# A four-layer graph network on one Trainium2 core: product banks in turn over the graphs' borders, a second buffer for the turned means, mask stores four graphs ahead

## What is computed

```python
adjT = jnp.transpose(adj.astype(jnp.float32), (0, 2, 1))
w = _masked_row_softmax(adjT)              # 1/degree on the edges, 0 elsewhere
region = jnp.matmul(w, features)           # features = h; mean of h over the edges
region = jnp.matmul(region, kernel_1) + bias_1
region = _batch_norm(region, gamma_1, beta_1)
people = jnp.matmul(jnp.transpose(w, (0, 2, 1)), region)
people = jnp.matmul(people, kernel_2) + bias_2
people = _batch_norm(people, gamma_2, beta_2)
x = x + people
```

## Time and profile before

| what | value |
|---|---|
| median of 3 runs | 1524.31 us (1522.05 to 1525.0) |
| profiled execution, its own time | 1522.59 us |
| its span, first to last instruction | 1520.8 us |
| TensorE matmuls busy | 1394.4 us (92%) |
| VectorE busy | 1148.9 us (76%) |
| ScalarE busy | 815.6 us (54%) |
| GpSimd busy | 383.4 us (25%) |
| granted TensorE clock, tenths, 40 slices of 38 us | `9999999799968989999999999999999999999998` |

### The profile page before, as it was taken

One profiled execution on the slowest core, in us unless ns is written; L12 is line 12 of the kernel. 1 busy time (PEld: TensorE's weight loads), 2 busy tenths in 40 slices (PEclk: granted clock), 3 DMA queues, 4 the chain that ended last, 5 costly groups with the idle time before them and its releaser, 6 DMA issues.

```text
span 1520.8 us, 32886 instructions
## 1 busy us (share of the span) xinstructions
PE 1394.4 (92%) x12642; PEld 1258.7 (83%) x12642; DVE 1148.9 (76%) x3270; ACT 815.6 (54%) x1811; POOL 383.4 (25%) x337
## 2 busy tenths in 40 slices
PE   5899999799945888999999999999999999999886
PEld 5899999555535777999999998999999999999785
DVE  4566664687835767888898888888888888887565
ACT  4677777022233454745656556556574565654621
POOL 6334340000010304133132331331313313223120
PEclk9999999799968989999999999999999999999998
DMA  9999992376742122231432323413323143131111
GB/s 206 227 207 213 206 220 64 102 251 234 246 157 56 48 79 84 71 91 52 109 105 64 98 60 99 114 50 105 91 84 92 51 110 105 50 84 46 39 42 43
DMA packets 111839, 169.35 MB, mean 111 GB/s; under 512 B 9808, under 2 KB 61760, under 8 KB 109632
## 3 DMA queue, kind: packets, MB, share of 16 engines
q1 hardware_dynamic: 87264, 125.20, 28.3%
q0 software_dynamic: 19584, 33.56, 12.0%
q10 hardware_dynamic: 4832, 8.45, 1.6%
HBM read 158.74 MB, written 42.00 MB: 132 GB/s over the span
## 4 chain that ended last, share of the span: by engine, by line
PE 46%; DVE 12%; DVEq 4%; ACT 3%; POOL 3%; issue 2%; DMA 0%; ACTq 0%
PE ps L1666 31%; PE ps L1625 3%; PE ps L1648 2%; DVE wts_C L973 2%; PE ps L1593 2%; PE ps L1637 2%; PE ps L1639 2%; PE ps L1638 2%; POOL wts_B L886 1%; DVEq L996 1%; PE ps L1679 1%; DVE xC L1050 1%; DVE wts_A L973 1%; DVEq L1006 1%; DVE st_B L908 1%
## 5 line engine op out<-in xcount | busy, mean ns | idle before, releaser
L1666 PE MATMUL ps<-hV,wts_B 128*128 128x129 f32 x2048 | 252.9, 279 | 13.2 <-POOL wts_B L886 5.4
L886 POOL TENSOR_TENSOR wts_B<-wts_B,off 128x1024 f32<-128x1024 f32 (+7 forms) x128 | 177.9, 1414 | 322.8 <-PE ps L1648 322.8
L1666 PEld LDWEIGHTS ps<-hV,wts_B 128*128 128x128 f32 x2048 | 241.6, 194 | 17.6 <-POOL wts_B L886 7.4
L1666 PE MATMUL ps<-hP_A,wts_A 128*128 128x129 f32 x1920 | 230.9, 275 | 1.2 <-ACT xB L1392 0.7
L1666 PEld LDWEIGHTS ps<-hP_A,wts_A 128*128 128x128 f32 x1920 | 221.5, 191 | 3.8 <-DVE hP_C L957 2.9
L1666 PE MATMUL ps<-hP_C,wts_C 128*128 128x129 f32 x1920 | 220.1, 274 | 0.0
L1666 PEld LDWEIGHTS ps<-hP_C,wts_C 128*128 128x128 f32 x1920 | 217.4, 191 | 0.5
L973 DVE SCALAR_TENSOR_TENSOR wts_A<-row_A,least_A,ring_A 128x1024 f32<-128x1024 f32 x128 | 161.0, 1275 | 11.3 <-ACT row_A L1347 7.7
L973 DVE SCALAR_TENSOR_TENSOR wts_C<-row_C,least_C,ring_C 128x1024 f32<-128x1024 f32 x120 | 167.0, 1404 | 0.0
L295 ACT ACTIVATE maskT<-ps 128x1024 fp8e4<-128x1024 bf16 x128 | 131.2, 1025 | 56.4 <-PE ps L337 45.2
L349 PE MATMUL ps<-x,adj_b 128*128 128x129 f16 x896 | 121.3, 223 | 15.8 <-ACT whn L278 13.3
(11 more groups left out here) (237 smaller groups left out, 2707.1 us busy)
## 6 DMA issues: line engine op xcount, KB each, us to landing
adj_b<-in_adj POOLq DMA_DIRECT2D x120, 256.0 KB, 10.0
maskT_scratch<-maskT SPq DMA_DIRECT2D x16, 1024.0 KB, 6.9
ring_A<-maskT_scratch SPq DMA_DIRECT2D x64, 256.0 KB, 3.1
off<-maskT_scratch SPq DMA_DIRECT2D x32, 512.0 KB, 6.6
ring_C<-maskT_scratch SPq DMA_DIRECT2D x64, 256.0 KB, 3.3
xa<-in_x SPq DMA_DIRECT2D x16, 512.0 KB, 4.5
whT_scratch<-whT_s ACTq DMA_DIRECT2D x32, 256.0 KB, 6.4
whT_b<-whT_scratch SPq DMA_DIRECT2D x16, 512.0 KB, 4.8
```

Source lines behind the costliest of these rows:

```text
L886: pool.tensor_tensor(w, w, off_fp8[:, k, k * P:N], ALU.mult).then_inc(S["B", "up"], 1)
L1666: last = nc.tensor.matmul(Q_SLOTS[c // 2 % 2][:, c % 2, 0:PW], wts[y][:, j, c * P:c * P + P], src[:, j, :], start=(j == 0), stop=(j == T - 1))
```

## The change

1. The bank of a product is (b * T + c) % 3, in turn over the graphs' borders, and line 343 asks for the division three tiles back everywhere.
2. The halves of the turned means go in turn into `whT_s` and into a second buffer, which is the part of `maskT` for the last two tiles of the last graph. Odd halves of the first 14 graphs use the second one; the last four halves all use `whT_s`. Each buffer has its own semaphore, and ScalarE waits for the last store from the second buffer before it writes the last graph's mask there.
3. SP issues the mask stores of graphs 0 to 3 at the start of the second stage, and then in `save(b)` that of graph b + 4. All on one semaphore, but for graph 0, which has its own.

```diff
-            BANK = [c % 3 for c in range(T)]
             LAG, HT = 3, T // 2
-            psW = [ps[:, 2 + BANK[c], :] for c in range(T)]
+
+            def psW(b, c):
+                return ps[:, 2 + (b * T + c) % 3, :]
...
+            SPARE = 2 * (B - 2)
+            by_spare = [n for n in range(SPARE) if n % 2 == 1]
+            by_own = [n for n in range(2 * B) if n not in by_spare]
+            whT_spare = maskT[:, B - 1, T - 2:T, :].rearrange("p t n -> p (t n)").bitcast(fp32)
...
                         act.wait_ge(a_sums_made, n + 1)
-                        if n > 0:
-                            act.wait_ge(a_whT_out, n * 16)
-                        nc.scalar.copy(whT_s[:, :], psWT[:, h * HALF:(h + 1) * HALF]).then_inc(a_whT_kept, 1)
+                        k, mine, kept = (1, by_spare, whT_spare) if n in by_spare else (0, by_own, whT_s[:, :])
+                        if mine.index(n) > 0:
+                            act.wait_ge(a_whT_out[k], mine.index(n) * 16)
+                        nc.scalar.copy(kept, psWT[:, h * HALF:(h + 1) * HALF]).then_inc(a_whT_kept, 1)
                         act.wait_ge(a_whT_kept, n + 1)
-                        act.dma_start(whT_dram[b, :, h * HALF:(h + 1) * HALF], whT_s[:, :]).then_inc(a_whT_out, 16)
+                        act.dma_start(whT_dram[b, :, h * HALF:(h + 1) * HALF], kept).then_inc(a_whT_out[k], 16)
...
                             act.wait_ge(a_turned, n + 1)
-
+                            if b == B - 1 and c == T - 2:
+                                act.wait_ge(a_whT_out[1], len(by_spare) * 16)
...
-                            if not (first and c < 3):
-                                pe.wait_ge(a_wh, n + 1 - (3 if c >= 3 else 2))
-                            q = psW[c]
+                            if n >= 3:
+                                pe.wait_ge(a_wh, n - 2)
+                            q = psW(b, c)
...
+            b_mask_first, b_mask_out = stage_sem("b_mask_first"), stage_sem("b_mask_out")
+            AHEAD = 4
...
                         if b == B - 1:
-                            sp.wait_ge(a_whT_out, 2 * B * 16)
+                            sp.wait_ge(a_whT_out[0], len(by_own) * 16)
...
+                    def save_mask(b):
+                        sp.dma_start(maskT_dram[b], maskT[:, b, :, :]).then_inc(b_mask_out if b > 0 else b_mask_first, 16)
+
+                    for b in range(AHEAD):
+                        save_mask(b)
+
                     def save(b, par):
-                        sp.dma_start(maskT_dram[b], maskT[:, b, :, :]).then_inc(b_mask_out[par], 16)
+                        if b + AHEAD < B:
+                            save_mask(b + AHEAD)
                         sp.wait_ge(b_pT, b + 1)
...
+                    sp.wait_ge(b_mask_out, (B - 1) * 16)
                     for par in range(2):
-                        sp.wait_ge(b_mask_out[par], B // 2 * 16)
                         sp.wait_ge(b_pT_out[par], B // 2 * 16)
```

More of the change, by code:

```diff
@@ L139, in gnn_stack_kernel @@
             (a_var, a_rstd, a_h, a_turned, a_kept, a_wh_made, a_deg,
-             a_wh, a_sums_made, a_whT_kept, a_whT_out) = (stage_sem(n) for n in (
+             a_wh, a_sums_made, a_whT_kept) = (stage_sem(n) for n in (
                 "a_var", "a_rstd", "a_h", "a_turned", "a_kept", "a_wh_made", "a_deg",
-                "a_wh", "a_sums_made", "a_whT_kept", "a_whT_out"))
+                "a_wh", "a_sums_made", "a_whT_kept"))
+            a_whT_out = [stage_sem(f"a_whT_out{k}") for k in range(2)]
+            SPARE = 2 * (B - 2)
+            by_spare = [n for n in range(SPARE) if n % 2 == 1]
+            by_own = [n for n in range(2 * B) if n not in by_spare]
+            whT_spare = maskT[:, B - 1, T - 2:T, :].rearrange("p t n -> p (t n)").bitcast(fp32)
             psT = [ps[:, k, :].bitcast(bf16) for k in range(2)]
-            BANK = [c % 3 for c in range(T)]
             LAG, HT = 3, T // 2
-            psW = [ps[:, 2 + BANK[c], :] for c in range(T)]
+            def psW(b, c):
+                return ps[:, 2 + (b * T + c) % 3, :]
             psG = ps[:, 5, 0:GW]
@@ L277, in divide @@
                         act.wait_ge(a_deg, b * T + c + 1)
-                        nc.scalar.mul(whn[:, c, 0:P], psW[c][:, 0:P], rdg[:, c:c + 1]).then_inc(a_wh, 1)
+                        nc.scalar.mul(whn[:, c, 0:P], psW(b, c)[:, 0:P], rdg[:, c:c + 1]).then_inc(a_wh, 1)
                     def keep_whT(b, h):
@@ L534, in gnn_stack_kernel @@
             pT_b = sbb("pT_b", [P, 2, N])
-            b_mask_out = [stage_sem(f"b_mask_out{k}") for k in range(2)]
+            b_mask_first, b_mask_out = stage_sem("b_mask_first"), stage_sem("b_mask_out")
+            AHEAD = 4
             b_pT_out = [stage_sem(f"b_pT_out{k}") for k in range(2)]
@@ L563, in _ @@
                             save(k * 2 + par, par)
-                    sp.wait_ge(b_mask_out[0], 16)
+                    sp.wait_ge(b_mask_first, 16)
                     sp.wait_ge(b_pT_out[0], 16)
```

## The result

The changed kernel takes **1506.88 us** (median of 4 runs, 1504.79 to 1508.29), the kernel before 1523.85 us on the same chip (median of 4 runs). The ratio is 0.9892, with a 95% interval of 0.9877 to 0.9906. Forecast were 1507.5 us, 1502 to 1514, and faster with a chance of 0.95: all three hold. The profiled execution took 1508.29 us (span 1506.5), 14.3 us less than that of before.

A forecast was written before the change was run, and what follows sets the result against it. TensorE was taken as the bound in both stages, leaving only its idle time and the stages' ends to win: 1522.59 - 13.3 - 2.5 = 1506.8, or 1508.5 by the median; forecast 1507.5 us, range 1502 to 1514.

The forecast's parts named there:

- First stage: TensorE's waits for ScalarE's division, mostly at graph borders, shrink: 16.1 - 2.8 - 0.4 + 0.4 = 13.3 us gained.
- TensorE only arrives earlier and waits longer: Second graph's 2.77 us wait at 42.86, where VectorE waits for x, stays; the 0.4 us border before it is lost.
- Part 1: Banks over the border: small gaps of 0.35 us go to zero; large ones, up to 2.30 us, keep 0.5 us.
- its mask copies have two banks of room: First stage: ScalarE, busy 125.57 of 160 us, was listed among checks of what is late next.
- Part 2: Second whT buffer: ScalarE's 11.5 us of store waits go, except the last, about 1.4 us, with what the banks leave.
- Start of the second stage: Graph 2's whT load, queued behind four mask stores (10 to 27.6 us), costs 0, with 2 us in the range.
- End of the second stage: Mask stores ahead free the last pTf store; VectorE is last and the next stage starts 2.5 us earlier.
- The transfers set the first stage's pace: Rival, chance 0.12: late x delays h and TensorE waits; 4.9 us of the gain lost, time 1512.4.
- The end is no shorter: Rival, chance 0.08: other transfers keep the queue full at the second stage's end, pTf lands unchanged; time 1510.0.
- The store queue slows the second stage: Rival, chance 0.02: each graph's transfers go one after another, 6.0 us a graph, 78 us over 13 graphs; 1585 in all.
- It does not do what it says: Rival, chance 0.03: first-stage border waits stay because a release other than the division ends them; time 1520 to 1523.
- which comes when it comes: Second graph's x transfer, for which VectorE sat 7.0 us; its landing was taken as given.

The follow-up runs named there:

- e2_buffer: Only the second buffer of the turned means, on the kernel before: 1512.37 us against 1523.12, ratio 0.9927.
- e3_masks: Only the mask stores issued four graphs ahead, on the kernel before: 1520.0 us against 1523.12, ratio 0.9982.
- w_late: Changed kernel with the weights' small loads moved behind the x load of graph 12, two x buffers: 1504.45 us against 1522.7, ratio 0.9874.
- w_last: Changed kernel with the weights' small loads moved behind the last x load of all, two x buffers: 1500.17 us against 1522.51, ratio 0.9848.
- e1_banks: Only the product banks in turn over the borders and the relaxed line 343, on the kernel before: 1518.27 us against 1523.12, ratio 0.997.
- ahead1: Changed kernel with mask stores issued one graph ahead instead of four: 1504.77 us, ratio 0.9889 to the kernel before.
- again: Second profiled execution of the changed kernel, nothing altered: 1502.97 us.
- ahead16: Changed kernel with all sixteen mask stores issued at the start of the second stage: 1524.42 us against 1522.42 for the kernel before, ratio 1.0013.

## Why the prediction was right, and where not

- **The sum** was -13.3 for the first stage, 0 for the second's start and -2.5 for its end, together -15.8; the profiled execution gave -12.1, +0.5 and -2.7, together -14.3. The forecast of 1507.5 against a median of 1506.88 is closer than its terms were, and in part luck: the four executions lie between 1504.79 and 1508.29, and the second profiled execution of the same kernel gives -13.9, -1.8 and -2.7.
- **First stage.** All of the gaps behind the stall went: 16.1 - 2.8 + 0.4 - 0.4 = 13.3 us, as worked out. "TensorE only arrives earlier and waits longer" was right. In this trace the wait ended 0.36 us later and the two tiles behind it took 5.41 us instead of 4.57, together 1.2 us. That is 13.3 - 1.2 = 12.1. In the second one it ended at 42.40, 0.46 us earlier than before, and the four tiles lost to the clock what they lost before, 1.6 us: 13.3 + 0.5 is near the 13.9 there. So the sum's base was the stall's end, which moves with the landing of x (41.2 before, 41.5 and 40.7 us after); the sum took it as fixed.
- **Part 1 failed**, though the sum held. It gave the relaxed bank "a tile (1.77 us)" of room in the large gaps, with 0.5 us left. The runs showed that it brings next to nothing there: with the banks alone the wait moved to the transposes (11.7 us in 12 times, longest 2.0). The large gaps were the buffer's loop. For the small gaps of 0.35 us the step was right, as e2_buffer shows, where only they are left. The line "its mask copies have two banks of room" looked at ScalarE's load and not at the order in which it works.
- **Part 2** was right and took more of the gain than its place in the text gave it: 8.4 of 12.1 us.
- **Start of the second stage.** The third load was not late; taking 0 for it was right, and the value nearer to 10 us for four stores than to 27.6 too (the last of them landed 16.2 us after the first was issued, at 2.4 to 3.5 us each). The 0.5 us is the first row product at the lower clock, 3.19 us against 2.68; in the second profiled execution it took 2.05 (granted clock 1.00), and the whole stretch 29.59 us. That is the clock noise of 1 to 2 us which the prediction allowed. The rule of the Trainium skill (DMA: Bandwidth & Descriptors, Queues, rings and completion order), that descriptors are consumed in ring order, agrees with the run with sixteen stores: the load landed 1.5 us behind the last of them and not before.
- **End of the second stage.** 2.5 forecast, 2.7 measured; VectorE is last, as said, and e3_masks gives the same by itself.
- **The rivals.** *The transfers set the first stage's pace* fell: behind the first graph's start (2.3 us for h, 2.8 before) no weight load waits for x or h but in the second graph, though the DMA share is at 1.05. Its ground against, that the 24.0 us belong to three loads in flight, was only part of it: without the small loads the same x took 16.1 us. How thin the cover is shows in the profiled execution of w_late, where an x issued some 16 us late cost 9.7 us. *The end is no shorter* fell by e3_masks. *The store queue slows the second stage* fell for four ahead: 300 to 400 us has TensorE busy 100.00 of 100. Its mechanism is real, but strikes once, at the start, as sixteen ahead show. *It does not do what it says* fell by the waits.
- Behind the stall with x, the prediction stopped at "which comes when it comes". Asking why it came so late would have found another 6.7 us (1506.88 to 1500.17; the ratios, 0.9892 and 0.9848, each to before on the same chip, give 6.7 us too).

## What to carry to other kernels

Where a wait ends at work that an engine does in order, follow that engine's queue back to its own first wait: the buffer at the root takes the large gaps away, and a relaxed wait further down, by itself, moves them to the next consumer. Look at what stands on the same queue ahead of a transfer that is late once: small loads that nobody needs yet belong behind the last one that somebody waits for. Of stores ahead of their time, issue as many as take the last one off the path, not all: a load on the same queue waits for each of them. And have a second trace of an unchanged kernel before you read a difference of 2 us from one.

## What was not expected of the hardware

- Sixteen loads of weights, together small, ahead on SP's queue made a 0.5 MB load with rows of 512 bytes land 24.4 us after issue; with them away it took 16.1 us, beside the same adjacency loads. Whether it is their number or the size of their packets was not tried apart.
- The median landing of x rose from 4.5 us to 12.2 and then 17.2 (13.1 and 10.3 in two more traces of the changed first stage) as the gaps of TensorE closed, while the DMA share from 66 to 226 us rose only from 0.99 to 1.05 and 1.06. The landings did not all grow. Before, the x loads issued up to 67 us took 11 to 24 us and the later ones 3.9 to 4.9; in the changed kernel the slow ones (14 to 24 us) last until 109 us; in w_last (14 to 18 us) until 173 us, and the two after that took 5.5 and 5.7. The adjacency loads landed late in the same time. So a shorter graph makes the slow time at the start last longer. That it is a backlog of adjacency loads which drains more slowly is argued, not shown.
- The lower clock behind a wait cost the same whatever the wait's length. Take the four tiles behind the stall, less the wait and less four tiles of 1.77 us: 1.6 us for waits of 2.20 (e1_banks), 2.77 (before), 3.16 (e3_masks), 3.73 (e2_buffer), 3.82 (ahead1), 3.97 (again), 4.70 (ahead16) and 9.69 us (w_late), and 2.6 us in one trace, that of the changed kernel with its wait of 4.03.
